# A four-layer graph network on one core: four joined changes, with the zeros of the late table rows written in 50 pieces

## What is computed

```
sage:  out = x @ w_self.T + segment_sum(w * x[src], dst) @ w_neigh.T; out / |out|
gcn1:  d = rsqrt(in-degree + 1);  h = relu(d * (sum over edges of d*(x@W1)[src] + own) + b1)
gcn2:  the same with W2 (128 -> 256 features)
hop:   two hops  h = 0.5 * (normalised weighted neighbour sum) + 0.5 * x;  relu(h) @ W.T + b
rel:   twice:  segment_sum(relu((x @ W[type])[src] + b[type]), dst)
```

## Time and profile before

| | us |
|---|---|
| median of 3 runs (2834.94 to 2842.83) | 2838.32 |
| the profiled execution, and its span | 2843.29; 2841.4 |
| PE (TensorE matmul) busy | 2525.3 |
| POOL (GpSimd) busy | 1726.6 |
| DVE (VectorE) busy | 1327.8 |
| ACT (ScalarE) busy | 561.7 |

### The profile page before, as it was taken

One profiled execution on the slowest core, in us unless ns is written; L12 is line 12 of the kernel. 1 busy time (PEld: TensorE's weight loads), 2 busy tenths in 40 slices (PEclk: granted clock), 3 DMA queues, 4 the chain that ended last, 5 costly groups with the idle time before them and its releaser, 6 DMA issues.

```text
span 2841.4 us, 44073 instructions
## 1 busy us (share of the span) xinstructions
PE 2525.3 (89%) x12873; PEld 2026.6 (71%) x12874; DVE 1327.8 (47%) x2836; ACT 561.7 (20%) x1659; POOL 1726.6 (61%) x1701
## 2 busy tenths in 40 slices
PE   6799999899898999999999997998788879987675
PEld 4598888788798988888777774665555546555454
DVE  7799988797322551111244233444333424433332
ACT  1355555555100000000011112111011121110000
POOL 5788878772067777774000004777777657777776
PEclk9899999999999999999999998999999989998888
DMA  3133333333698779945444434555454545554343
GB/s 98 50 146 149 151 142 128 121 143 140 207 295 281 241 250 349 314 151 158 134 133 150 134 118 135 161 155 154 133 150 148 148 131 160 155 148 113 115 115 100
DMA packets 208107, 454.85 MB, mean 160 GB/s; under 512 B 52672, under 2 KB 141870, under 8 KB 207818
## 3 DMA queue, kind: packets, MB, share of 16 engines
q1 hardware_dynamic: 56004, 257.55, 26.0%
q0 software_dynamic: 66944, 111.48, 14.9%
q10 hardware_dynamic: 84998, 83.76, 8.7%
HBM read 285.85 MB, written 166.80 MB: 159 GB/s over the span
## 4 chain that ended last, share of the span: by engine, by line
PE 54%; POOL 27%; issue 13%; DMA 3%; DVE 2%; ACT 1%; ACTq 1%; PEldq 0%; DVEq 0%; POOLq 0%; PEld 0%; SPq 0%
PE agg L980 29%; POOL edges_bucketed L665 16%; POOL gathered L720 12%; PE agg L1028 10%; PE y L819 10%; PE prod L804 2%; DMA gathered<-table_rel,idx_rel 1%; DMA edges_bucketed<-edges,pos_u 1%; PE agg L884 1%; ACTq L1259 1%; PE turn_ps L789 0%; ACT turned L1079 0%; PE y L860 0%; DMA table_rel<-y_sb 0%; DVE relw L1494 0%
## 5 line engine op out<-in xcount | busy, mean ns | idle before, releaser
L720 POOL DMA_INDIRECT gathered<-table_rel,idx_rel x840 | 810.6, 965 | 696.5 <-ACTq L1259 443.8
L1028 PE MATMUL agg<-gathered,onehot 128*128 x2464 | 617.1, 407 | 137.5 <-SPq L620 81.6
L1028 PEld LDWEIGHTS agg<-gathered,onehot 128*128 128x128 f32 x2464 | 492.0, 204 | 266.5 <-issue 197.2
L665 POOL DMA_INDIRECT edges_bucketed<-edges,pos_u x416 | 507.0, 1219 | 148.1 <-issue 124.0
L980 PE MATMUL agg<-t_sb,stream 128*128 128x128 f32 (+1 forms) x3750 | 562.8, 312 | 14.6 <-issue 7.6
L980 PEld LDWEIGHTS agg<-t_sb,stream 128*128 128x128 f32 x3750 | 526.2, 193 | 48.4 <-issue 14.8
L1794 DVE SCALAR_TENSOR_TENSOR onehot<-iota,keybase,edges 128x256 f32<-128x256 f32 x616 | 278.1, 483 | 592.2 <-PE agg L1028 482.7
L704 POOL DMA_INDIRECT edges_parted<-parted,pos_u x416 | 402.0, 966 | 180.2 <-issue 126.1
L819 PE MATMUL y<-relw,turned 128*128 128x512 f32 x600 | 283.2, 617 | 74.1 <-ACT turned L1094 41.4
L884 PE MATMUL agg<-h_sb,stream 128*128 128x257 f32 x1250 | 338.5, 396 | 0.0
L860 PE MATMUL y<-gathered,relw 128*128 128x128 f32 x1300 | 238.8, 293 | 41.1 <-DVE t_sb L1511 15.2
(11 more groups left out here) (198 smaller groups left out, 1740.3 us busy)
## 6 DMA issues: line engine op xcount, KB each, us to landing
table_rel<-y_sb ACTq DMA_DIRECT2D x200, 256.0 KB, 2.9
stream<-counts_dense SPq DMA_DIRECT2D x50, 832.0 KB
stream<-weights_dense SPq DMA_DIRECT2D x50, 832.0 KB
stream<-counts_dense SPq DMA_DIRECT2D x50, 768.0 KB
stream<-weights_dense SPq DMA_DIRECT2D x50, 768.0 KB
table_rel<-zeros ACTq DMA_DIRECT2D x2, 12800.0 KB, 92.6
weights_dense<-stream SPq DMA_DIRECT2D x25, 832.0 KB, 3.4
counts_dense<-t_sb SPq DMA_DIRECT2D x25, 832.0 KB, 5.2
```

Source lines behind the costliest of these rows:

```text
L665: pool.indirect_dma_start(recs_dram, bass.IndirectOffsetOnAxis(ap=pos_u[0:rows, c:c + 1], axis=0), edges[0:rows, c, :], None).then_inc(s_s ...
L720: pool.indirect_dma_start(gathered[:, slot * D:(slot + 1) * D], None, tables[n], bass.IndirectOffsetOnAxis(ap=idx_rel[:, c:c + 1], axis=0) ...
L1028: mm = pe.matmul(agg[b][:, 0:D], onehot[:, half_ * QUAD + k, :], gathered[:, bass.ds(((q + quads0) & (GQ - 1)) * (QUAD * D) + k * D, D)], ...
```

## The change

All of it is joined in one program:

1. **Block stage.** `iota` is copied once into the fourth PSUM bank by a matmul with the identity, and the one-hots read it there. Two banks go round for the blocks. VectorE evicts only groups 2 and 4 of each half, ScalarE all others; ScalarE's weighing and layer steps are dealt out between its groups, and VectorE makes both one-hots of the next half before its first eviction.
2. **Counts in bf16.** `c_block` and `counts_dense` are bf16. The tables of gcn1 and gcn2 are split in three bf16 pieces that add up to the fp32 value (`split_rows`); one bf16 matmul of 384 columns takes the place of the fp32 one of 128; VectorE adds the three sums (`add_pieces`). The table of gcn1 is split in five groups of five tiles, four of them at the end of the block stage, ahead of the flag, the fifth after it.
3. **Order of gcn2.** The product runs two tiles behind and comes before the turn; VectorE's part runs three behind; the multiplication by d moves behind the product. The tail has no order of its own.
4. **Loads and parting.** The biases are loaded at the start, the relation weights after hop1's streams. The parting steps stand at tiles 3, 7 and 9 of gcn1 (before: 0, 6, 8), in other memory; the parted edges are loaded behind hop2's stream of tile 4.
5. **Zeros.** ScalarE issues one piece of 512 KB at the start of each of the 50 halves, in place of the two transfers.

```diff
-    BANKS = 3
+    BANKS = 2
+    EVICTS = [group in (2, 4) for h in range(HALVES) for group in range(len(GROUPS[h % 2]))]
...
-        c_dram = dram("counts_dense", (NPAD, NPAD))
+        c_dram = dram("counts_dense", (NPAD, NPAD), BF16)
...
-        c_block = t_sb[:, LANE:2 * LANE]
+        c_block = t_sb[:, LANE:LANE + LANE // 2].bitcast(BF16)
...
-        built_ps = y_ps[1:]
+        built_ps = y_ps[1:3]
+        iota_ps = y_ps[3][:, 0, 0:P]
...
...
+            load_biases(rel_b0, 0)
+            load_biases(rel_b1, 1)
...
+                    if n == "hop2" and t == 4:
+                        sp.wait_ge(s_parted, 1)
+                        sp.dma_start(kept, parted_dram.rearrange("(p c) f -> p c f", p=P)).then_inc(s_kept, 16)
...
+            for n in DENSE[2:]:
+                stream_blocks(n, w_dram, half)
+                if n == "hop1":
                     load_relations(sp, rel_w0, 0, REL, s_wrel[0])
...
+            pe.wait_ge(s_picked, RANKED)
+            pe.matmul(iota_ps, ident[:], iota[:], start=True, stop=True).then_inc(s_iota, 1)
...
+                            if split:
+                                mm = pe.matmul(sums(n, t)[:, 0:3 * HID], half_counts(at, part)[:, place],
+                                               pieces[n][:, s, :, :].rearrange("p k d -> p (k d)"),
+                                               start=s == 0, stop=s == TILES - 1)
...
+                static_tiles(dense_visits("gcn2", split),
+                             [(2, lambda t, b: rows_product("gcn2", t, [w2_sb[:]])),
+                              (1, lambda t, b: turn("gcn2", halves[0:1], t))])
...
+            def clear_rows(i):
+                late_rows = tables[RELS[i // TILES]][EARLY * NPAD:REL * NPAD].rearrange("(p c) d -> p c d", p=P)
+                piece = slice(i % TILES * EARLY, (i % TILES + 1) * EARLY)
+                act.dma_start(late_rows[:, piece, :], zeros[:].unsqueeze(1).broadcast_to([P, EARLY, D])
+                              ).then_inc(s_zeroed, 16)
...
+                if i < HALVES:
+                    clear_rows(i)
+                groups = len(GROUPS[i % 2])
+                each = -(-(HALF + 1) // (groups - 1))
+                for group in range(groups):
+                    if i < HALVES and evicted_by(groups_until(i) + group)[0] == 0:
+                        evict(i, group)
+                    layer_part(i, group)
+                    if group >= 1 and i + 1 < HALVES:
+                        weigh(i + 1, (group - 1) * each, group * each)
...
-            for n in RELS:
-                late_rows = tables[n][EARLY * NPAD:REL * NPAD].rearrange("(p c) d -> p c d", p=P)
-                act.dma_start(late_rows, zeros[:].unsqueeze(1).broadcast_to([P, EARLY * TILES, D])).then_inc(s_zeroed, 16)
...
-                        to, iota[:].unsqueeze(1).broadcast_to([P, width, P]),
+                        to, iota_ps.unsqueeze(1).broadcast_to([P, width, P]),
...
+                step(nc.vector.tensor_copy(first, rows))
+                step(nc.vector.tensor_tensor(rest, rows, first, ALU.subtract))
+                step(nc.vector.tensor_copy(second, rest))
+                step(nc.vector.tensor_tensor(third, rest, second, ALU.subtract))
...
+            SPLITS = {2 * TILES + 2: (0,), 2 * TILES + 4: (1,), 2 * TILES + 5: (2, 3)}
...
+                if i in SPLITS:
+                    for group in SPLITS[i]:
+                        split_first(group, prep)
...
             step = Steps(dve, s_dense, 0, 0)
+            split_first(4, step)
...
+            def add_pieces(n, t):
+                step(nc.vector.tensor_tensor(post[:, 0:HID], sums(n, t)[:, 0:HID], table(n, t), ALU.add))
+                for k in (1, 2):
+                    step(nc.vector.tensor_tensor(post[:, 0:HID], sums(n, t)[:, k * HID:(k + 1) * HID], post[:, 0:HID],
+                                                 ALU.add))
...
-            static_tiles(None, [(2, gcn2_product), (1, gcn2_rows)],
-                         [(1, gcn2_rows), (2, gcn2_product), (1, gcn2_product)])
+            static_tiles(None, [(1, gcn2_rows), (3, gcn2_product)])
```

More of the change, by code:

```diff
@@ L565, in _ @@
                     for part in range(2):
-                        for at in range(groups_until(2 * t + part + 1))[-2:]:
-                            who, done = evicted_by(at)
-                            sp.wait_ge(evicted[who], done)
+                        for done, n in zip(evicted, evicted_until(groups_until(2 * t + part + 1))):
+                            sp.wait_ge(done, n)
                         sp.dma_start(dense(w_dram, t, part), half(t, part)).then_inc(w_stored[t % 2][part], 16)
@@ L962, in _ @@
                 pe.sem_inc(s_passed, 1)
-            def dense_visits(n):
-                at0, width = TILES * (DENSE.index(n) + 1), WIDTH[n]
-                def visits(t):
-                    at = at0 + t
-                    if n == "gcn1" and t == 3:
-                        pe.wait_ge(s_early, 5)
-                        pe.matmul(early_ps[0], lower_b[:], early, start=True, stop=True)
-                        pe.matmul(early_ps[1], ones_b[:], early, start=True, stop=True).then_inc(s_early_mm, 1)
-                    for part in range(2):
-                        if part == 0:
-                            pe.wait_ge(sum_free, at + 1)
-                        pe.wait_ge(s_stream[at % 2][part], 16 * ((at - TILES) // 2 + 1))
-                        for s in range(*PARTS[part]):
-                            if t == 0:
-                                pe.wait_ge(S[BEFORE[n], "table_ready"], s + 1)
-                            mm = pe.matmul(sums(n, t)[:, 0:width], stream[:, at % 2, s * P:(s + 1) * P], table(n, s),
-                                           start=s == 0, stop=s == TILES - 1)
-                        mm.then_inc((half_free, sum_ready)[part], 1)
-                return visits
+                gcn(split=False)
+            with pe.Else():
+                gcn(split=True)
             def hop2_turn(t, b):
@@ L995, in rel1b_turn @@
                 turn("rel1b", halves, t)
[L997 to L1000 removed]
+            parts = {"hop1": [],
                      "hop2": [(1, hop2_turn), (3, hop2_relations), (2, lambda t, b: turn_normed("hop2", t, b)),
```

232 lines of the change are left out of this document (138 added, 94 removed).

## The result

The changed kernel takes **2733.9 us** (median of 4 runs, 2730.5 to 2737.4) against 2836.8 for the kernel before beside it: ratio 0.963, 95% interval 0.961 to 0.965, 3.7% faster. The forecast was 2738, range 2710 to 2768. The profiled execution took 2734.9 us, its span 2733.1, which is 108.3 less than before, where the working said 100.7.

What follows compares the result with a forecast made beforehand. TensorE was taken to bound the kernel, with GpSimd's held-up scatters a second limit in the block stage. The terms summed to -100.7 us, 2742.6 for the profiled execution and 2738 for the median, range 2710 to 2768.

Steps and rivals of the forecast that it cites:

- Block pace: Block stage: ranks in PSUM free GpSimd's scatters, so a tile takes 23.2 us instead of 24.2; -24 us, bounds 0 and -30.
- the rival in which GpSimd stays held up: Block stage: any long one-hot holds GpSimd, not the second SBUF input; -24 becomes 0, 2762 us; chance 0.10.
- End of the block stage: VectorE splits four table groups there, 2.8 us each, so the flag comes +8.0 us later; bounds +3 and +11.
- First load: From the flag to gcn1's first multiplication: the load has half the bytes; -1.7 us.
- gcn1, -33: gcn1: bf16 multiplications take 4.12 us a tile, with 4 us of stalls from parting; 110 us instead of 143.1.
- Gap, gcn2 and tail: Gap between gcn1 and gcn2 goes, -7; gcn2 at 4.85 us a tile, -48; tail with two more products, +2.
- Hops: hop1 unchanged, 0; hop2's stream at tile 5 lands as due behind the parted edges, +2 us, bounds 0 and 15.
- Held in gcn1 by casts and subtractions: gcn1: split copies and subtractions hold the second scatter, hop2 stands some 14 us more; 2752 us; chance 0.08.
- VectorE at 5.6 us a tile in gcn2: gcn2: VectorE is the bound because the wait for ScalarE's root isn't covered; +19, 2757 us; chance 0.07.
- Late evictions: Block stage: ScalarE's evictions stand behind weighings with only two banks; 173 us more, 2911 us, slower than before; chance 0.04.

Runs made afterwards that it cites:

- e1: Changed kernel with the one-hots reading the ranks from SBUF again instead of PSUM; 4103.5 us on a slow chip, ratio 0.986 to the kernel before.
- e5: The same kernel as e1, run again, on such a slow chip too; 4107.7 us.
- e9: The kernel of e1 a third time (ranks in SBUF), scatters beside the block stage; 2748.7 us, ratio 0.968 to the kernel before.
- e3: Changed kernel with fp32 counts, no table splits and fp32 multiplications of 128 columns in gcn1 and gcn2; 4170.5 us on a slow chip.
- e12: The kernel of e3 again (fp32 counts, no splits), on a slow chip too; 4167.2 us.
- e2: Changed kernel with the zeros in two 13 MB transfers behind gcn2 instead of 50 pieces; 4115.8 us on a slow chip.
- e7: Changed kernel with VectorE evicting groups 1, 3 and 5 of each half, the first between its two one-hots; 2795.3 us, ratio 0.985 to the kernel before.
- e4: Changed kernel with gcn2's old order (turn, then product) and the bf16 multiplication kept; 4138.3 us on a slow chip, ratio 0.991 to the kernel before.
- e8: Changed kernel with the fourth group split behind the flag and hop2's parted edges loaded two tiles later; 2721.1 us, ratio 0.958 to the kernel before.
- e11: On top of e8: two splits in VectorE's idle time, three behind the flag, parting spread, parted edges loaded later; 2712.7 us, ratio 0.956 to the kernel before.
- e6: The changed kernel itself, unedited, run again beside e7 and e8; 2730.7 us, ratio 0.962 to the kernel before.
- e10: The kernel of e2 again (zeros in two transfers), scatters beside the block stage; 2732.7 us, ratio 0.963 to the kernel before.

## Why the prediction was right, and where its terms were off

**Block pace, -24, measured -39.2: mis-sized, by two steps.** "Where TensorE sets the pace, seven tiles took 160.8 us (155.35 to 316.15), 22.97 each" was the first. TensorE did not set it alone. In the changed kernel, which has no wait for an eviction, the same seven tiles take 157.9 us, 22.55 each: 0.42 less (1.7 us of waits for evictions by ScalarE are named in them). The busy share already said so: over the longer stretch of the earlier trace rows TensorE was busy 294.44 of 300 us, which is 0.43 us a tile of standing. The whole stage runs at 22.59 (at 22.55 in e1 to e5). The second was "I allow 0.2 us a tile for late ones": there are none. ScalarE is busy 15.2 us a tile, near the 16.6 worked out. And I gave the whole gain to the ranks in PSUM. e9 splits it: from 581.3 to 559.0 us without them, by the new dealing of the evictions and what comes with it (two banks, the dealt-out steps of ScalarE; no run takes these apart), and 17.3 more by them. The bf16 counts and the pieces of zeros have no part in it: the stage takes 541.3 us in e3 and e12 without the one and in e2 without the other, as in e1. So the rival in which GpSimd stays held up was priced too high as well: it gives about 2749, not 2762. e7 shows that the dealing carries as much weight: with two banks and another dealing the stage takes 600.8 us, more than before the change.

By the Trainium skill, SBUF — State Buffer, Who interferes with whom, a VectorE instruction with two SBUF inputs contends with a GpSimd instruction that reads SBUF, one with a single input, outside the two-port modes, doesn't. The pair of e1 and e4 agrees: 2.05 against 0.96 us.

**End of the block stage, +8, measured +10.8.** The step that failed is "by width that is 0.5 and 0.83": the cast of 640 columns to bf16 took 0.79 to 0.82 us. A group is 3.4 us, two of them 6.8 instead of 5.6. The mechanism was right: e8 and e11 take back 3.6 and 9.1 us by taking groups from ahead of the flag.

**First load, -1.7, measured +1.7.** The load became shorter as said, 4.1 us from its issue to the first multiplication instead of 5.5. The step that failed is that I took SP's way from the flag to its first issue as unchanged: it was 4.6 us, not 1.5. In every trace SP has read the flag and reached its branch 0.92 us behind it. The next instruction of SP comes 0.5 us after that branch in the kernel before and 3.6 in the changed one, where the streams of gcn1 and gcn2 stand on both sides of the branch. With that program the issue came 4.0 to 5.2 us after the flag in all twelve experiments, those without splits (e3, e12) among them, so it isn't VectorE's. Why the branch takes longer stays open. The term as a whole varies with it: in e6 to e11 the way from the flag to the first multiplication is 7.4 to 9.4 us.

**gcn1, -33, measured -33.9.** The stalls came at tiles 8 and 10 as worked out, 0.5 and 3.0 us, and e11, which spreads the parting, removes the second. The lower clock behind it, 1.7 us, was in no term; a tile of 4.06 us instead of 4.12 made up for it.

**Gap, gcn2 and tail, -53, measured -52.4.** A tile takes 4.6 us at first and mostly 4.83 to 4.98 where VectorE is the limit, forecast 4.85. The tail was off: 10.0 us from the end of the last multiplication to hop1 (944.07 to 954.10) instead of 4.1 and my +2, since two products wait 4.20 and 2.66 us for VectorE's hand-over of the one bank. The first two tiles, which have no product beside them and take 4.1 us, made up for part of it. e4 shows the order to be worth 20 us, e12 the pieces 32. No run takes back the moved loads alone; that the gap is gone is read from the trace.

**Hops, +2, measured +7.4.** The parted edges were scattered at 1292.5, and the stream of tile 5, which stands behind their load, came 4.6 us late (5.8 and 6.4 in e6 and e10). I had 2 us for the wait, and nothing for what follows it: TensorE then ran its next tile at a lower granted clock (0.76 from 1300 to 1307 us), 1.8 to 2.9 us more.

**The rivals.** GpSimd held up: shown not to be so, by e1 against e4, and by scatters that end at 558 us. Held in gcn1 by casts and subtractions: the second scatter has a mean of 0.97 us, as before. VectorE at 5.6 us a tile in gcn2: 4.9. Late evictions: not in the changed kernel, but e7 shows that another dealing of the same two banks has them.

## What to carry to other kernels

A pace taken from a stretch "where the engine is the limit" has to be cleared of that engine's own idle share in that stretch first. On a path that one engine paces, price a wait at its length and then at what the engine loses in the clock behind it; and look for the idle time of the helper engine into which a preparing step fits, before putting it ahead of something that others wait for. Look at what stands ahead of an eviction in its engine's order, and not at the busy share alone.

## What the runs showed of the hardware

**A short wait lowers TensorE's granted clock, but not always.** Behind waits of 3.04, 3.04 and 3.05 us in gcn1 the clock was 0.76 for 7 us (changed kernel), 1.00 (e6, the same program) and 0.70 for 10 us (e8), that is 1.2 GHz for part of it: the 15 tiles behind the wait took 62.8, 61.3 and 64.0 us. It stayed at 1.00 in e9 and e10 too, where they took 61.1, and was 0.76 again in e7. Behind the longer waits of 4.6 to 6.4 us in hop2 it fell in each of the changed kernel, e6 and e10.

**Where instructions come slowly.** On the chips of e1 to e5 and e12 the other engines stood for long while GpSimd scattered. Timeline of e1 in gcn1, TensorE's instructions beside the second scatter:

```profile
1327.45 0.48 PE L968 MATMUL agg<-gathered,stream 128*128 128x384 bf16 x1 [2.32 <-issue]
...
1333.05 0.48 PE L968 MATMUL agg<-gathered,stream 128*128 128x384 bf16 x1 [2.31 <-issue]
...
1352.32 2.42 PE L968 MATMUL agg<-gathered,stream 128*128 128x384 bf16 x7 [18.79 <-issue]
```

A multiplication is recorded every 2.8 us, and then come 18.8 us in which TensorE waits for nothing that the profile can name; the long wait comes again every 70 us until the scatters end at 1816 us, and behind them gcn2 ran at its full 4.7 us a tile. The scatters themselves kept 0.96 us in the median. Why this was so on two chips and not on the others was not tried. The changed kernel itself did not run there. The nearest, e2, which differs in the zeros alone, had ratio 0.988 (0.982 to 0.994) to the kernel before: 1.2% ahead, where the change gives 3.7% elsewhere.
